# Ends of the attention layers of a four-layer gated block: order of the statistics, two batches' rows on GpSimd, clears in the tile loop

## What is computed

```python
x = x + tanh(g_xattn[0]) * L0_xattn(layernorm(x), ctx, ctx, ...)
x = x + tanh(g_ffn[0])   * L0_ffn(layernorm(x), ...)      # router, best of 8 experts (128x128)
x = x + tanh(g_xattn[1]) * L1_xattn(layernorm(x), ctx, ctx, mask, ...)   # q, k, v layer normed
x = x + tanh(g_ffn[1])   * L1_ffn(layernorm(x), ...)      # best 2 of 8 experts, 512 wide
x = x + tanh(g_xattn[2]) * L2_xattn(layernorm(x), ctx, ctx, ...)         # 64 wide heads, causal
x = x + tanh(g_ffn[2])   * L2_ffn(layernorm(x), ...)      # latent attention, then best 2 of 8
x = x + tanh(g_xattn[3]) * L3_xattn(layernorm(x), ctx, ctx, mask, ...)   # rotary
x = x + tanh(g_ffn[3])   * L3_ffn(layernorm(x), ...)      # one expert chosen for a batch

def layernorm(x):
    m, v = mean(x, -1), var(x, -1)
    return (x - m) / sqrt(v + 1e-5)
```

## Time and profile before

| | |
|---|---|
| median of 3 runs | 1052.25 us (1049.93 to 1054.67) |
| span of the profiled execution | 1057.6 us |
| PE busy | 919.4 us, 87% |
| DVE busy | 785.7 us, 74% |
| ACT busy | 557.7 us, 53% |
| POOL busy | 490.0 us, 46% |
| weights of PE loaded (PEld) | 655.6 us, 62% |

### The profile page before, as it was taken

One profiled execution on the slowest core, in us unless ns is written; L12 is line 12 of the kernel. 1 busy time (PEld: TensorE's weight loads), 2 busy tenths in 40 slices (PEclk: granted clock), 3 DMA queues, 4 the chain that ended last, 5 costly groups with the idle time before them and its releaser, 6 DMA issues.

```text
span 1057.6 us, 19542 instructions
## 1 busy us (share of the span) xinstructions
PE 919.4 (87%) x6337; PEld 655.6 (62%) x6337; DVE 785.7 (74%) x2080; ACT 557.7 (53%) x1494; POOL 490.0 (46%) x451
## 2 busy tenths in 40 slices
PE   6898985888778999869997598988989999989987
PEld 4787533767578989727775243434437677768774
DVE  6889999999756777769998376777734744589982
ACT  4675456886444445724443156766764233445533
POOL 5444553555066564635556777574530600024430
PEclk9999896999879999969999659989999999999998
DMA  9300000000111111410000322222102000000001
GB/s 324 149 1 1 2 6 1 1 1 1 41 39 39 41 40 33 109 66 1 0 1 0 107 67 62 82 76 62 31 1 101 1 1 1 1 2 2 1 1 40
DMA packets 29828, 40.55 MB, mean 38 GB/s; under 512 B 11468, under 2 KB 25036, under 8 KB 29228
## 3 DMA queue, kind: packets, MB, share of 16 engines
q1 hardware_dynamic: 27244, 34.28, 10.3%
q0 software_dynamic: 2496, 5.16, 1.9%
HBM read 31.44 MB, written 7.82 MB: 37 GB/s over the span
## 4 chain that ended last, share of the span: by engine, by line
PE 27%; issue 14%; POOL 7%; DVE 5%; ACT 3%; SPq 1%; DMA 0%; DVEq 0%; POOLq 0%; ACTq 0%
POOL att L1787 6%; PE ps L1163 4%; PE ps L829 4%; PE ps L1135 4%; PE ps L819 4%; PE ps L1147 3%; PE ps L793 1%; PE ps L1249 1%; PE ps L1257 1%; DVE rs L2124 1%; PE ps L1101 1%; DVE stats L2001 0%; SPq L570 0%; PE ps L1106 0%; DVE U L2029 0%
## 5 line engine op out<-in xcount | busy, mean ns | idle before, releaser
L1787 POOL TENSOR_TENSOR att<-att,ri 128x1232 f32<-128x1232 f32 x64 | 169.3, 2645 | 190.5 <-DVE ri L2130 190.5
L793 PE MATMUL ps<-VW,PT 128*128 128x128 f32 (+3 forms) x1280 | 157.6, 278 | 17.5 <-DVE x L2145 16.0
L793 PEld LDWEIGHTS ps<-VW,PT 128*128 128x128 f32 (+1 forms) x1280 | 148.4, 192 | 35.2 <-DVE x L2145 28.3
L1369 ACT ACTIVATE PT<-ps 128x512 f32<-128x512 f32 x128 | 70.6, 594 | 89.5 <-PE ps L766 88.7
L766 PE MATMUL ps<-W,att 128*128 128x128 f32 (+1 forms) x640 | 86.9, 282 | 16.2 <-POOL att L1787 14.7
L1761 POOL TENSOR_TENSOR rstd<-ve,minus_half 128x4 f32<-128x4 f32 x38 | 38.8, 1039 | 114.2 <-DVE ve L2016 97.7
L900 PE MATMUL ps<-PT,att 128*128 128x128 f32 x624 | 80.8, 285 | 8.5 <-issue 8.4
L829 PEld LDWEIGHTS ps<-U,att 128*128 128x128 f32 x512 | 66.3, 191 | 33.1 <-issue 29.1
L766 PEld LDWEIGHTS ps<-W,att 128*128 128x128 f32 (+1 forms) x640 | 72.7, 143 | 22.3 <-POOL att L1787 15.5
L2581 DVE CUSTOM_DVE_ANT_0 C<-ps,cmaskb 128x512 bf16<-128x512 f32 (+1 forms) x128 | 71.1, 555 | 20.7 <-PE ps L1135 18.0
L2581 DVE CUSTOM_DVE_ANT_0 U<-ps,cmaskb 128x384 bf16<-128x384 f32 (+1 forms) x128 | 53.9, 421 | 41.8 <-PE ps L1135 41.5
(11 more groups left out here) (432 smaller groups left out, 2105.6 us busy)
## 6 DMA issues: line engine op xcount, KB each, us to landing
U<-in_ffn SPq DMA_DIRECT2D x1, 6176.0 KB, 23.2
U<-split SPq DMA_DIRECT2D x144, 32.0 KB
W<-split SPq DMA_DIRECT2D x144, 32.0 KB
W<-in_packed SPq DMA_DIRECT2D x1, 2162.5 KB, 23.5
U<-in_ffn SPq DMA_DIRECT2D x1, 2060.0 KB, 9.7
U<-in_moe SPq DMA_DIRECT2D x1, 2048.0 KB, 7.3
split<-VBD SPq DMA_DIRECT2D x4, 384.0 KB, 2.9
split<-W SPq DMA_DIRECT2D x4, 384.0 KB, 2.7
```

The costliest lines, as they stand in the source:

```text
L793: q = mm(attended(s, t), PT[0:m, t.slot(2), c, :], batch(VW, t.group)[0:m, c * D:(c + 1) * D], start=(c == 0), stop=(c == NC - 1))
L1369: go(PT[:, t.slot(2), 4 * k:4 * k + 4, :].rearrange("p c n -> p (c n)"), ps[:, k0 + k, :], ACT.Copy).then_inc(probsT, 1)
L1787: tt(p, p, over_keys(ri[:, t.slot(2), :]), ALU.mult).then_inc(probs, 1)
```

## The change

1. `early_moments`: batches 0 and 1 now both follow the update of tile 13, which is behind the row sums and reciprocals of tile 15; batch 2 still follows the update of tile 14, and behind it come the stats and aggregates of three tiles of batch 3 (`aggregate`). Behind the last update, `moments` does the fourth tile only (`ready=TB - 1`). This holds for the ends of X0, X1, X2 and X3.
2. In F0 and F1, the rows of batches 0 and 1 are normed by POOL: `normed_rows` there does root 0, four `tensor_scalar`, root 1, four `tensor_scalar`, root 2, root 3. DVE norms batches 2 and 3 only, and waits for POOL's eight rows ahead of batch 2.
3. ACT's four clears of VW go from between the copies of the turned rows into the experts' tile loop, behind `scale0` of tiles 2 to 5.
4. Four semaphores of chains on DVE (e0_chain, m_rec, rope_chain, sel_chain) become one, vector_chain, with offsets.

```diff
@@ ACT, F0
             for b in range(B):
                 turned_copy(F0, b, 0, [(FT[:, cols(b)], None, None)])
-                go(VW[:, b, :, :], ident.unsqueeze(1).to_broadcast([P, NC, D]), ACT.Copy, scale=0.0).then_inc(zeros_set, 1)
...
+            def clear_values(b):
+
+                go(VW[:, b, :, :], ident.unsqueeze(1).to_broadcast([P, NC, D]), ACT.Copy, scale=0.0).then_inc(zeros_set, 1)
...
                 elif t == 1:
                     copy_wT(0)
+                if 2 <= t < 2 + B:
+                    clear_values(t - 2)
@@ POOL
+            def normed_rows(s):
+
+                for b in range(B):
+                    root(ROUND0[s] + b, b)
+                    if b < AHEAD:
+                        pool.wait_ge(s_rstd, ROUND0[s] + b + 1)
+                        for k in range(b * TB, (b + 1) * TB):
+                            pool.tensor_scalar(xn1[:, k, 0:D], x[:, k, :], mv[:, k, 0:1], rstd[:, k:k + 1],
+                                               ALU.subtract, ALU.mult).then_inc(s_xn, 1)
...
-            roots(F0)
+            normed_rows(F0)
...
-            roots(F1)
+            normed_rows(F1)
@@ DVE
-            def moments(n, src, b, rms=None, rows=P, of_rows=None):
-
+            def aggregate(n, src, b, tiles, rows=P):
 
                 counted = n - (B if n >= ROUND0[MLA] + B else 0)
-                for i in range(TB):
+                for i in tiles:
                     v.bn_stats(stats[0:rows, b * TB + i, :], src(i)).then_inc(s_stats, 1)
-                dve.wait_ge(s_stats, TB * (counted + 1))
-                for i in range(TB):
+                dve.wait_ge(s_stats, TB * counted + tiles.stop)
+                for i in tiles:
                     v.bn_aggr(mv[0:rows, b * TB + i, :], stats[0:rows, b * TB + i, :]).then_inc(s_aggr, 1)
-                dve.wait_ge(s_aggr, TB * (counted + 1))
+                dve.wait_ge(s_aggr, TB * counted + tiles.stop)
+
+            def moments(n, src, b, rms=None, rows=P, of_rows=None, ready=0):
+
+
+                aggregate(n, src, b, range(ready, TB), rows)
...
-                    moments(ROUND0[s] + b, rows_of(x, b), b)
+                    moments(ROUND0[s] + b, rows_of(x, b), b, ready=TB - 1 if first else 0)
...
                     if s in (F0, F1):
+                        if b == AHEAD:
+                            dve.wait_ge(s_xn, TB * (ROUND0[s] + AHEAD))
                         if b >= AHEAD:
                             normed_rows(s, b)
...
                 def early_moments(t):
 
-                    if isinstance(t.n, int) and 0 <= t.n - (NT - TB) < EARLY:
-                        b = t.n - (NT - TB)
+                    if not isinstance(t.n, int) or t.n < NT - 3:
+                        return
+                    for b in {NT - 3: (0, 1), NT - 2: (2,)}.get(t.n, ()):
                         dve.wait_ge(x_new, XNEW0[s] + (b + 1) * TB)
                         moments(ROUND0[s + 1] + b, rows_of(x, b), b)
-                        if s in (X0, X1) and b == EARLY - 1:
-                            for n in range(AHEAD):
-                                normed_rows(s + 1, n)
+                    if t.n == NT - 2:
+                        dve.wait_ge(x_new, XNEW0[s] + NT - 1)
+                        aggregate(ROUND0[s + 1] + B - 1, rows_of(x, B - 1), B - 1, range(TB - 1))
```

More of the change, by code:

```diff
@@ L94 @@
 RINGS = 3
+OUT_CHAIN = (E - HALF - 1) * NT
+ROPE_CHAIN = OUT_CHAIN + UNITS
+SELECT_CHAIN = ROPE_CHAIN + 2 * B
 HOLD = 4
@@ L373, in build @@
         side_ps, side_sb, offset_set = sem("side_ps"), sem("side_sb"), sem("offset_set")
-        rot_ps, rope_chain, roped = sem("rot_ps"), sem("rope_chain"), sem("roped")
+        rot_ps, roped = sem("rot_ps"), sem("roped")
         y_set, tables_set, scratch = sem("y_set"), sem("tables_set"), sem("scratch")
@@ L385, in build @@
         qk_ps, qk_max, kq_ps, kq_exp = map(sem, ("qk_ps", "qk_max", "kq_ps", "kq_exp"))
-        diag_set, pv_ps, oT_sb, m_rec = map(sem, ("diag_set", "pv_ps", "oT_sb", "m_rec"))
+        diag_set, pv_ps, oT_sb = map(sem, ("diag_set", "pv_ps", "oT_sb"))
         first_ps, k_flat, q_flat, k_chain, q_chain, k_split, q_split = map(
@@ L391, in build @@
         stacked = [sem(f"stacked{r}") for r in range(HOLD)]
-        e0_ps, e0_scaled, e0_added, e0_pair, e0_half, e0_chain = map(
-            sem, ("e0_ps", "e0_scaled", "e0_added", "e0_pair", "e0_half", "e0_chain"))
+        e0_ps, e0_scaled, e0_added, e0_pair, e0_half = map(
+            sem, ("e0_ps", "e0_scaled", "e0_added", "e0_pair", "e0_half"))
+        vector_chain = sem("vector_chain")
         up_ps, silu, gated, down_ps = map(sem, ("up_ps", "silu", "gated", "down_ps"))
-        pol, pol_sb, sel_done, sel_chain = sem("pol"), sem("pol_sb"), sem("sel_done"), sem("sel_chain")
+        pol, pol_sb, sel_done = sem("pol"), sem("pol_sb"), sem("sel_done")
         h3_ps, h3_sb, r3_ps, r3_sb, o3_ps = map(sem, ("h3_ps", "h3_sb", "r3_ps", "r3_sb", "o3_ps"))
@@ L2485, in add_scaled @@
                 tt(x[:, t, :], x[:, t, :], hsum[:, t % 2, :], ALU.add).then_inc(x_new, 1)
-            c = Chain(dve, e0_chain)
+            c = Chain(dve, vector_chain)
             for t in range(NT + 1):
@@ L2589, in beside @@
                         .rearrange("p i g (m d) -> p i g m d", m=2)
-                    v.reciprocal(rec[:, :, :, :].unsqueeze(4), o[:, :, :, :, HD:VE]).then_inc(m_rec, 1)
-                    dve.wait_ge(m_rec, n + 1)
+                    v.reciprocal(rec[:, :, :, :].unsqueeze(4), o[:, :, :, :, HD:VE]).then_inc(vector_chain, 1)
+                    dve.wait_ge(vector_chain, OUT_CHAIN + n + 1)
                     half = o_s[:, b * TB:(b + 1) * TB, c * (D // 2):(c + 1) * (D // 2)]
@@ L2633, in _ @@
             mix_and_moments(B - 1)
-            roping = Chain(dve, rope_chain)
+            roping = Chain(dve, vector_chain, ROPE_CHAIN)
             def rope3(b):
@@ L2660, in _ @@
             dve.wait_ge(pol, 2)
-            c = Chain(dve, sel_chain)
+            c = Chain(dve, vector_chain, SELECT_CHAIN)
             lg = ps[:, 7, 0:B * E].rearrange("p (b e) -> p b e", e=E)
```

## The result

The changed kernel takes 1058.2 us (median of 20 runs, 1054.7 to 1062.2) beside 1052.1 for the kernel before (20 runs) on the same chip: ratio 1.0061, interval 1.0046 to 1.0075. It is 0.6% slower. The forecast was 1048.8 in a range to 1053.2, "slower" had 0.08: number, sign and range were wrong.

The account below looks back on a forecast made before the run. No one engine was taken to bound the kernel, but hand-overs at the stage ends; gains of 1.15 (X0), 0.5 (X1), 0.8 (X2) and 1.0 (X3) sum to 3.45 us, giving 1048.8 us, range 1045.8 to 1053.2.

Parts of the forecast that it names:

- slower: Rival: GpSimd takes two passes for the two-column form, 0.94 us a row; the kernel loses 5.9 us, 1058.1; chance 0.08.
- What bounds the ends: Ends of X0 to X3: no one engine bounds; stages hand work on, and an edit is worth what it removes there.
- d: Time of one GpSimd norm row of 128x128 in F0 and F1: 0.33 us taken, bounds 0.23 and 0.47.
- The formula around it: End of X0: GpSimd's queue, roots and eight rows, then DVE's last four norms, ends at 111.25 + 8d.
- X1: End of X1: GpSimd's queue ends at 264.05 + 8d against 267.2; 0.5 us gained at d = 0.33.
- the sum: Whole kernel: gains at the ends of X0, X1, X2 and X3, 1.15 + 0.5 + 0.8 + 1.0 = 3.45 us.
- more than summed: Rival: shorter idle times bring TensorE's clock back sooner behind the ends, 3 us more gained, 1045.8; chance 0.15.
- The clears: ACT's clears moved behind scale0 of tiles 2 to 5: one scaling 0.35 us late, cost zero or at most 0.4.
- X2: End of X2: earlier row sums gain zero; three tiles' statistics taken from behind the last update gain 0.8 us.
- X3: End of X3: 0.2 us from product 14's shorter wait and 0.8 from statistics, 1.0 us in all.
- The lock between DVE and GpSimd: The two engines' instructions can block each other; batch 1's variance may wait for a new GpSimd row, up to d.
- the turning point: Row time on GpSimd at which the whole change turns from gain to loss: d = 0.58.

Follow-up runs that it names:

- second profile of before: The kernel before, unchanged, run and profiled again: 1053.3 us against 1051.2, ratio 1.002; the profile's span is 1050.9 us.
- shorter rows: Changed kernel with a tensor_tensor for each of GpSimd's eight tensor_scalar rows, mean not subtracted: 1046.5 us, 0.9928 of the kernel before.

## Why the prediction was wrong

By its own steps:

1. **What bounds the ends: right.** Row sums, last variance and last update (111.06 said, 111.24 measured) came as forecast. Product 14 waits 0.18 for ACT instead of 0.39 for DVE, and the shift against the second profile of before goes from +0.17 us at product 13 to 0.0 at the last update: the 0.2 us forecast.

2. **d, the term that failed.** 0.33 was taken, 0.23 to 0.47 was allowed, 0.78 was measured. The formula around it was good: 111.25 + 8 * 0.78 = 117.5 for batch 3 of F0, measured 118.06. For X1 it gives 3.15 - 8 * 0.78 = -3.1; measured, the norm of F1 is another 3.7 us late (8.3 less the 4.6 of F0's gate), 3.4 of them behind the last update. With 0.78 in it the sum gives a loss of 2.0 + 3.1 less 1.8, thus 3.3 us: 1055.6, already outside the range. The error was in the choice of rows. The line through 4 and 1232 elements joined a small float32 instruction to a conversion of bytes, and its slope of 0.82 ns was carried to float32. The two-operand row on the same 128x128, 0.47, was taken as an upper bound although it does one operation and the new form two. An upper bound would have had to be two passes, and that stood in the text as the rival, with 0.08, put aside because "subtract and multiply are cheap". It is this rival that came, with 0.94 for 0.78, and its 1058.1 is the measured 1058.2. That hit is partly luck: its d was too high and the next point was missing in it too.

   The Trainium skill (GPSIMD Engine Reference, Engine selection) said that elementwise work belongs on VectorE, and the run agrees: 0.78 against DVE's 2.14 / 8 = 0.27 us for the same row. Its "roughly line-rate" with one input doesn't hold for this form: the slope of 3.5 ns measured here is more than twice the 1.5 ns that one estimates from the same page's best case (Elementwise — side-by-side cycle accounting), 1.8 cycles at 1.2 GHz.

3. **What was missing: TensorE's wait and its clock.** I followed GpSimd's queue to batch 3, since that ended last, and not to batch 1, whose rows TensorE needs right behind its first turn. At d = 0.33 the rows of batch 1 would have been done in time; at 0.78 they end at 114.8, and TensorE, done with turn 0 since 112.3, waits 2.55 us. The prediction had the last routing end "near 117.0 even at the slower clock"; it ends at 120.45 + 3.42 = 123.87. The rival "more than summed" had the mechanism, with the opposite sign only: that shorter idle times bring the clock back. The small matmuls between the turns show its price, 3.6 us of the kernel's time (1.0061 to 1.0027); in the traces the gates stand 1.9 and 2.5 us closer to the last updates. By the trace the norms end 2.7 + 3.4 = 6.1 us late and the gates wait 1.9 + 3.0 = 4.9 us more; with 0.4 in X1, less the gains of X2 and X3 (1.7 and 1.0) and the 1.8 of F3's clock, this is 6.9 us, within the 4.8 to 7.9 of the ratio. How much of it is the clock varies from one execution to the next: the second profile of before has its gate of F1 7.1 us behind the update, where other kernels with the same norms have up to 9.8.

4. **The clears: right.** Four copies without clears; the scaling of tile 4 comes 0.23 us late (0.35 said) and the next one is back on its time; SP's copies run from 143.28 for 21.87 us, and the product of X1 that needs them doesn't wait for them. Zero by experiment.

5. **X2: right in kind, low.** 0.8 was forecast; the early statistics gave 0.78 and the order of the row sums 0.67 more. I had argued that products 14 and 15 follow one another on TensorE, but the row sums, and GpSimd's last normalise behind them, also came 1.5 us earlier (shift 10.3 beside 11.8 in the loop), and the last product ended sooner for it: DVE's last update, which waited 2.23, waits 0.64 with its extra work in front and stands 0.67 sooner.

6. **X3: right.** 0.24 for the order (0.2 said) and 0.71 for the statistics (0.8 said): 0.95 against 1.0. What the sum had nothing for is the clock behind it: F3's first matmuls ran at 2.4 GHz and not at 1.2 GHz, worth 1.8 us, nearly twice the term itself. It isn't shown that the change causes this.

7. **The lock between DVE and GpSimd: right, and small.** Batch 2's variance lasted 0.37 instead of 0.17 beside the rows. The chance of it, up to d, had been left out of the sum.

The chances were the second mistake. Where one unmeasured instruction stands eight times in a queue that ends last, and the turning point (0.58) lies between the value taken and a rival's value that nothing in the rows excludes, 0.08 is too little.

## What to carry to other kernels

A price for an instruction that the trace doesn't show comes from a row with the same types, the same number of operations and a near size; two rows of other kinds can't be joined to a line. Before work is moved to an engine with other work behind it, follow its queue to the first consumer and not only to the last one, and ask what TensorE does meanwhile: an idle time of 2.55 us there went with a gate 4.6 us late, one of 3.27 with 6.3, partly by the lower clock behind it. If the turning point lies within what is unknown, halve the work that is moved: one batch instead of two had the moved order without the loss (1.0004), though without a gain too.

## What the runs showed of the hardware

- GpSimd's tensor_scalar with two float32 operations costs 3.5 ns an element between 32 and 512 elements and some 0.35 us besides (0.78 us at 128x128 in the changed kernel, 0.90 beside DVE's norms); constants in place of columns save little (1.92 for 2.15 us at 128x512); with one operation and one column it is 0.60 us at 128x128, a tensor_tensor there 0.37 to 0.45. A conversion of bytes to bfloat16 took 1.0 ns an element.
- One of the 128x128 instructions with constants lasted 2.66 us instead of 0.64 to 0.75 while DVE ran four tensor_tensors of 128x512 in 2.48 us. The Trainium skill (SBUF — State Buffer, Who interferes with whom) says that a VectorE instruction with two SBUF inputs contends with a GpSimd instruction that reads SBUF, and calls the shared port pair an exclusive lock; the trace agrees.
- TensorE's granted clock stayed at 2.4 GHz behind an idle time of 1.10 us (F0, one batch) and fell to 1.2 GHz behind 1.57, 2.27, 2.55, 3.27 and 3.29 us. But it also fell behind 0.51 us (F1, shorter rows), and in F0 of the kernel before, in the window from 118 us, with no idle time over 0.6 us since X0's last product. So the one wait doesn't tell when it falls; what else does is open. Small matmuls in the gaps kept it at 1.00 in both stages each time, at least up to the last group.
- The same four matmuls of 128x512 in F3 took 3.78 us at a granted 0.50 and 1.98 at 1.00.
